# Attention scores on four 64x64 tiles of the TensorE array, with exchanged token quarters

## The reference, cut to what matters

```python
xn = _layernorm(x, axis=-1)
q = q * cos + _rotate_half(q) * sin          # positions 0..255 inside a batch
k = k * cos + _rotate_half(k) * sin
scores = jnp.einsum('bhsd,bhtd->bhst', q, k) / jnp.sqrt(jnp.float32(D))
causal = jnp.triu(jnp.full((S, S), -jnp.inf, dtype=jnp.float32), k=1)
probs = jax.nn.softmax(scores + causal[None, None], axis=-1)
out = jnp.einsum('bhst,bhtd->bhsd', probs, v)
...
g = _silu(_L0_ffn_ref(xn, ...))
x = x + s * g
```

## Time and profile before

| | |
|---|---|
| median of 3 runs | 303.01 us (302.92 to 303.16) |
| the profiled execution | 303.29 us, its span 301.5 us |
| TensorE matmul busy | 289.6 us, 96% of the span |
| ScalarE busy | 239.3 us, 79% |
| VectorE busy | 229.7 us, 76% |
| GpSimd busy | 213.5 us, 71% |
| granted TensorE clock | 1.00 of full speed |

### The profile page before, as it was taken

One profiled execution on the slowest core, in us unless ns is written; L12 is line 12 of the kernel. 1 busy time (PEld: TensorE's weight loads), 2 busy tenths in 40 slices (PEclk: granted clock), 3 DMA queues, 4 the chain that ended last, 5 costly groups with the idle time before them and its releaser, 6 DMA issues.

```text
span 301.5 us, 8603 instructions
## 1 busy us (share of the span) xinstructions
PE 289.6 (96%) x2362; PEld 235.0 (78%) x2362; DVE 229.7 (76%) x909; ACT 239.3 (79%) x863; POOL 213.5 (71%) x325
## 2 busy tenths in 40 slices
PE   8798999999999999999999989999999999999994
PEld 2576888888888888777776779999977778887663
DVE  4889998987777898988898723444377889898981
ACT  4278789898887889989998676677787898999971
POOL 2478878697778669999999982333226899998730
PEclk9999999999999999999999999999999999999999
DMA  6864685879333233444333382000234243543410
GB/s 192 249 133 115 114 276 148 205 194 300 87 75 68 60 75 83 107 101 102 90 97 90 112 245 55 2 0 2 66 93 108 64 113 99 121 106 109 113 37 17
DMA packets 39596, 33.35 MB, mean 111 GB/s; under 512 B 4801, under 2 KB 36674, under 8 KB 39554
## 3 DMA queue, kind: packets, MB, share of 16 engines
q1 hardware_dynamic: 38098, 30.51, 39.8%
q0 software_dynamic: 1024, 2.10, 2.4%
q10 hardware_dynamic: 432, 0.23, 0.3%
HBM read 11.07 MB, written 4.98 MB: 53 GB/s over the span
## 4 chain that ended last, share of the span: by engine, by line
PE 64%; POOL 14%; DVE 9%; issue 6%; DMA 3%; ACT 1%; POOLq 0%; SPq 0%; DVEq 0%; ACTq 0%
PE bank L1199 9%; PE bank L1187 9%; PE bank L1216 8%; PE bank L1450 7%; PE bank L1438 6%; PE bank L1233 6%; POOL probs L499 5%; POOL staged L488 5%; PE bank L1161 3%; DVE rot_out L617 3%; PE bank L1218 3%; PE bank L1189 3%; POOL xn L515 3%; DMA qk_sb<-staged 3%; DVE masked L633 2%
## 5 line engine op out<-in xcount | busy, mean ns | idle before, releaser
L975 ACT ACTIVATE pexp<-masked,negmax 128x128 f32<-128x128 f32 (+1 forms) x256 | 113.9, 452 | 2.2 <-DVE negmax L633 2.2
L499 POOL TENSOR_SCALAR probs<-pexp,rden 128x128 f32<-128x128 f32 (+1 forms) x195 | 84.3, 447 | 27.0 <-DVE rden L640 25.2
L633 DVE CUSTOM_DVE_ANT_0 masked<-bank,mask 128x128 f32<-128x128 f32 (+1 forms) x256 | 75.9, 352 | 21.4 <-PE bank L1189 20.5
L488 POOL TENSOR_TENSOR staged<-rot_out 128x512 f32<-128x512 f32 x56 | 71.4, 1278 | 16.2 <-DVE rot_out L617 15.6
L617 DVE TENSOR_TENSOR rot_out<-bank,rot 128x1024 f32<-128x1024 f32 x64 | 77.7, 1215 | 4.6 <-PE bank L1163 3.5
L997 ACT COPY probsT<-bank 128x384 f32<-128x384 f32 x126 | 54.0, 480 | 27.3 <-PE bank L1199 26.0
L1199 PE MATMUL bank<-ident,probs 128*128 128x128 f32 x384 | 54.0, 275 | 0.7 <-issue 0.5
L975 ACT ACTIVATION_READ_ACCUMULATOR pexp<-masked,negmax 128x1 f32 x256 | 50.0, 195 | 0.0
L1187 PE MATMUL bank<-qk_sb 64*128 64x256 f32 x256 | 47.0, 428 | 1.7 <-DMA qk_sb<-staged 1.3
L1199 PEld LDWEIGHTS bank<-ident,probs 128*128 128x128 f32 x384 | 43.0, 140 | 3.4 <-issue 1.2
L1233 PE MATMUL bank<-vo_sb,ctxT 128*128 128x128 f32 x256 | 37.8, 278 | 0.7 <-ACT ctxT L1004 0.7
(11 more groups left out here) (117 smaller groups left out, 483.6 us busy)
## 6 DMA issues: line engine op xcount, KB each, us to landing
qk_sb<-staged SPq DMA_DIRECT2D x128, 128.0 KB
w_sb<-in_w SPq DMA_DIRECT2D x2, 1024.0 KB, 5.8
w_sb<-in_w SPq DMA_DIRECT2D x4, 512.0 KB, 5.3
sorted_x<-z SPq DMA_DIRECT2D x1, 1408.0 KB, 8.0
sorted_g<-z SPq DMA_DIRECT2D x1, 1152.0 KB, 5.5
out<-res SPq DMA_DIRECT2D x8, 128.0 KB, 2.3
x_sb<-in_x SPq DMA_DIRECT2D x3, 256.0 KB, 3.8
rot<-in_c_rot SPq DMA_DIRECT2D x1, 512.0 KB, 5.7
```

The lines of the kernel that those rows point to most:

```text
L488: pool.tensor_tensor(staged[:, n % 2, :, m % 2, :], rot_out[:, m % 2, :, 0:S], rot_out[:, m % 2, :, S:2 * S], op=ALU.add).then_inc(staged_ ...
L499: pool.tensor_scalar(probs[:, g % 2, i, c], pexp[:, g % 2, i, c], rden[:, g % 2, i, k:k + 1], 1.0, ALU.mult, ALU.mult).then_inc(probs_read ...
L633: t = dve.tensor_tensor_reduce(masked[:, g % 2, i, c], s_bank[i][:, c], mask[:, c], -1.0, -NEG * 1e8, ALU.add, ALU.min, negmax[:, g % 2, i ...
L975: e = act.activation(pexp[:, g % 2, i, c], masked[:, g % 2, i, c], ACT.Exp, bias=negmax[:, g % 2, i, k:k + 1], scale=-1.0, accum_out=rowsu ...
```

## The change

The queries of each token tile are cut in quarters of 64 tokens, and the second tile's two quarters change places everywhere: `TOKEN_ORDER` says that positions 0 to 255 of a batch hold tokens of the quarters 0, 1, 3, 2. The rotary table and the mask follow that order, `x` is loaded and the result stored through it (`quarter_rows`), and softmax and sums over keys don't depend on it. `scores(g)` for g > 0 then issues five parts for each of the two heads in place of two, each on a 64x64 tile of the array: the row half is the head, the column half is the quarter's place in its tile. Column half 0 gets quarters 2 and 0 of the positions, with 256 and 64 keys; column half 1 gets quarters 3 and 1, with 128 + 64 and 128 keys (`SCORE_PARTS`). So each tile of the array streams 320 columns, where it was 384. What is left unwritten in PSUM is masked. Step 0 keeps the old form.

```diff
+Q = P // 2
+TOKEN_ORDER = (0, 1, 3, 2)
+SCORE_PARTS = ((2, slice(0, S)), (3, slice(0, P)), (1, slice(0, P)), (3, slice(P + Q, S)), (0, slice(0, Q)))
...
-    ang = np.arange(S, dtype=f)[None, :] * np.tile(inv, HPG)[:, None]
+    token = (np.array(TOKEN_ORDER)[:, None] * Q + np.arange(Q)).reshape(-1)
+    ang = token.astype(f)[None, :] * np.tile(inv, HPG)[:, None]
...
+        def quarter_rows(dram, part):
+            q = dram.rearrange("b (q p) c -> p b q c", p=Q)
+            return q[:, :, part::3 - 2 * part][:, :, 0:2]
...
                 def rows_in(u):
-                    n = slice(*TURNS[u])
-                    sp.dma_start(x_sb[:, n, :], xv[:, n, :]).then_inc(x_in[u], 16)
+                    for b in range(TURNS[u][0] // 2, TURNS[u][1] // 2):
+                        for part in range(2):
+                            sp.dma_start(x_sb[part * Q:part * Q + Q, 2 * b:2 * b + 2, :],
+                                         quarter_rows(x, part)[:, b]).then_inc(x_in[u], 16)
...
             def store(k):
...
-                sp.dma_start(out[b].rearrange("(n p) c -> p n c", p=P),
-                             res[:, k % 2].rearrange("p (n c) -> p n c", c=C)).then_inc(out_done[k % 2], 16)
+                for part in range(2):
+                    sp.dma_start(quarter_rows(out, part)[:, b],
+                                 res[part * Q:part * Q + Q, k % 2].rearrange("p (n c) -> p n c", c=C)
+                                 ).then_inc(out_done[k % 2], 16)
...
-                for i, r in enumerate(half_rows):
-                    wait(pe, masked_ready, 2 * g - 1 + i if g else 0)
-                    pe.matmul(s_bank[i][:, P:SW], qk_sb[r, 0, p, P:S], qk_sb[r, 1, p, :], start=True, stop=True)
-                for i, r in enumerate(half_rows):
-                    m = pe.matmul(s_bank[i][:, 0:P], qk_sb[r, 0, p, 0:P], qk_sb[r, 1, p, 0:P], start=True, stop=True)
+                for k, (q, keys) in enumerate(SCORE_PARTS):
+                    c = half_rows[q % 2]
+                    at = q // 2 * P
+                    for i, r in enumerate(half_rows):
+                        if k == 0:
+                            pe.wait_ge(masked_ready, 2 * g - 1 + i)
+                        m = pe.matmul(s_bank[i][c, at + keys.start:at + keys.stop], qk_sb[r, 0, p, q * Q:q * Q + Q],
+                                      qk_sb[r, 1, p, keys], start=True, stop=True)
                 m.then_inc(scores_done, 1)
```

More of the change, by code:

```diff
@@ L100, in host_constants @@
         "c_ident": np.eye(P, dtype=f),
-        "c_mask": np.where(k[None, :] > k[:, None], f(NEG), f(0.0)).astype(f),
+        "c_mask": np.stack([np.where(q[None, :] > q[:, None], f(NEG), f(0.0)) for q in (token[:P], token[P:])], 1).astype(f),
         "c_before": (k[:, None] < k[None, :]).astype(f),
@@ L391, in start @@
             def start():
-                xv = x.rearrange("b (n p) c -> p (b n) c", p=P)
                 def rows_in(u):
-                    n = slice(*TURNS[u])
-                    sp.dma_start(x_sb[:, n, :], xv[:, n, :]).then_inc(x_in[u], 16)
+                    for b in range(TURNS[u][0] // 2, TURNS[u][1] // 2):
+                        for part in range(2):
+                            sp.dma_start(x_sb[part * Q:part * Q + Q, 2 * b:2 * b + 2, :],
+                                         quarter_rows(x, part)[:, b]).then_inc(x_in[u], 16)
                 rows_in(0)
@@ L406, in start @@
                         sp.dma_start(rot[:], c_rot).then_inc(rot_in, 16)
-                sp.dma_start(mask[:, 0:P], c_mask).then_inc(m_in, 16)
-                sp.dma_start(mask[:, 2 * P:3 * P], c_mask).then_inc(m_in, 16)
+                sp.dma_start(mask[:, 0:P], c_mask[:, 0, :]).then_inc(m_in, 16)
+                sp.dma_start(mask[:, 2 * P:3 * P], c_mask[:, 1, :]).then_inc(m_in, 16)
                 sp.dma_start(wv_sb, w_vup).then_inc(w_in, 16)
@@ L477, in _ @@
             for i in range(2):
-                sp.wait_ge(out_done[i], 16 * B // 2)
+                sp.wait_ge(out_done[i], 32 * B // 2)
         @block.gpsimd
@@ L656, in stats @@
                 tiles = range(*TURNS[u])[first:last]
-                dve.wait_ge(x_in[u], 16)
+                dve.wait_ge(x_in[u], 16 * (TURNS[u][1] - TURNS[u][0]))
                 for n in tiles:
@@ L841, in add_rows @@
                 k = FINAL_ORDER.index(b)
-                wait(dve, out_done[k % 2], 16 * (k // 2))
+                wait(dve, out_done[k % 2], 32 * (k // 2))
                 dve.tensor_tensor(res[:, k % 2], gated[:], x_sb[:, 2 * b:2 * b + 2, :].rearrange("p n c -> p (n c)"),
@@ L1184, in scores @@
                 pe.wait_ge(qk_in[p], 32 * (g // NP) + 32)
-                for i, r in enumerate(half_rows):
-                    wait(pe, masked_ready, 2 * g - 1 + i if g else 0)
-                    pe.matmul(s_bank[i][:, P:SW], qk_sb[r, 0, p, P:S], qk_sb[r, 1, p, :], start=True, stop=True)
-                for i, r in enumerate(half_rows):
-                    m = pe.matmul(s_bank[i][:, 0:P], qk_sb[r, 0, p, 0:P], qk_sb[r, 1, p, 0:P], start=True, stop=True)
+                if g == 0:
+                    for i, r in enumerate(half_rows):
+                        pe.matmul(s_bank[i][:, P:SW], qk_sb[r, 0, p, P:S], qk_sb[r, 1, p, :], start=True, stop=True)
+                    for i, r in enumerate(half_rows):
+                        m = pe.matmul(s_bank[i][:, 0:P], qk_sb[r, 0, p, 0:P], qk_sb[r, 1, p, 0:P], start=True, stop=True)
+                    m.then_inc(scores_done, 1)
+                    return
+                for k, (q, keys) in enumerate(SCORE_PARTS):
+                    c = half_rows[q % 2]
+                    at = q // 2 * P
+                    for i, r in enumerate(half_rows):
+                        if k == 0:
+                            pe.wait_ge(masked_ready, 2 * g - 1 + i)
+                        m = pe.matmul(s_bank[i][c, at + keys.start:at + keys.stop], qk_sb[r, 0, p, q * Q:q * Q + Q],
+                                      qk_sb[r, 1, p, keys], start=True, stop=True)
                 m.then_inc(scores_done, 1)
```

## The result

| | before | after |
|---|---|---|
| median | 302.97 us (302.43 to 303.73, 6 runs) | 305.71 us (305.48 to 305.95, 6 runs) |
| profiled execution, span | 303.29, 301.5 | 305.83, 304.1 |

The change made the kernel slower: ratio 1.0091, 95% interval [1.0076, 1.0106]. The forecast was 300.1 us, its range 297.3 to 304.5.

What follows compares the result with a forecast made beforehand. TensorE was taken to lead the chain except where GpSimd holds it (113 to 165 us, gather stage). Terms -2.4 - 0.14 - 0.14 - 0.7 - 0.4 + 0.5 + 0.35 = -2.9 gave 300.1 us, range 297.3 to 304.5.

Steps and rivals of the forecast that it cites:

- The score group: TensorE's score matmuls of one step: 0.71 us in place of 0.85, 0.14 us less per step.
- rival 1: GpSimd's stretches: the gain goes on there; 295.1 us if all 63 groups count, 297.6 with half the held ones; a tenth.
- rival 3: Score groups: column halves with matmuls of unlike length don't run side by side; 0.92 us per group, 305.8 to 308.3; 0.15.
- rival 4: Score groups: TensorE's queue can't issue forty in 0.6 us; group of 1.1 to 1.2 us, over 315 us; 0.05.
- The sum of the score terms, -3.8: All score groups counted on the chain, without the transfers' fixed costs of 0.85 us: 3.8 us saved.
- forecast 2.4: Steps 5 to 22, 33 to 103 us: 18 groups at 0.14 are 2.52, less 0.1 lost to VectorE, so -2.4 us.
- rival 2: Early stretch: VectorE or transfers take up between half and all of the 2.4 us; 301.8 to 303.0 us; a tenth.
- forecast 0.7 and 0.14: Steps 42 to 46 save 5 x 0.14 = 0.7 us; of steps 40 and 41, before the experts, one group counts, 0.14.
- The gather stage to 280 us: 0: GpSimd's gathers, from 235.42 us to 280.57: GpSimd has no waits to give back, so nothing gained or lost.
- the start, +0.5: First loads of `x`, weights and rotary table: later by the halved transfers' extra issues, +0.5 us, bounds 0 and +1.0.
- The later loads of x ... 0: SyncE's queue: nine more issues, about 0.5 us each, on a queue that waits for GpSimd there; cost 0.
- the end, +0.35: Last store: the second half goes out one issue later with half the bytes; +0.35 us, bounds 0.2 and 0.5.

Runs made afterwards that it cites:

- experiment 15: Experiment 3's kernel unchanged (whole transfers, eight matmuls on 64x64 tiles, short part last), as control on another chip: 299.19 us, 0.9882 of the kernel before.
- experiment 10: Experiment 3's kernel once more (whole transfers, eight matmuls on 64x64 tiles in all steps), on another chip: 302.39 us, 0.9989 of the kernel before.
- experiment 4: The changed kernel with the old four score matmuls from step 42 on: 303.84 us, 1.0033 of the kernel before.
- experiment 12: Experiment 8's kernel once more (64x64 tiles, gathers replaced by additions, gates not brought back), on another chip: 300.40 us, 0.9917 of the kernel before.
- experiment 3: The kernel before with eight score matmuls per step on 64x64 tiles, query rows exchanged only in PSUM and put back by the transposes, whole transfers: 302.30 us, 0.9987.
- experiment 9: The changed kernel once more, on another chip: 305.42 us, 1.0095 of the kernel before.
- experiment 18: The changed kernel once more, on one more chip: 305.57 us, 1.0107 of the kernel before.
- experiment 1: The changed kernel with the four score matmuls of before, keeping the token order and halved loads and stores: 305.12 us, 1.007 of the kernel before.
- the mixed form: Experiment 3's kernel with the four matmuls of before in steps 46 to 61, the 64x64 form in all others: 300.18 and 299.95 us on two chips.
- experiment 2: The kernel before with only the ten score matmuls of the change, leaving out some scores; transfers and token order as before: 302.74 us, 0.9992.
- experiment 11: Experiment 5's kernel once more (form of before in steps 46 to 61), on another chip: 299.95 us, 0.991 of the kernel before.
- experiment 5: Experiment 3's kernel with the four matmuls of before in steps 46 to 61, the 64x64 form in all others: 300.18 us, 0.9908 of the kernel before.
- experiment 8: Experiment 3's kernel with each gather replaced by an addition on GpSimd, gates not brought back: 300.69 us, 0.9923 of the kernel before.
- experiment 13: Experiment 3's kernel with its four parts in the other order, so the 256-key matmul raises the semaphore: 299.53 us, 0.9876 of the kernel before.
- experiment 14: Experiment 3's kernel with one more matmul per step, on a 64x128 tile, that raises the semaphore: 314.61 us, 1.0381 of the kernel before.
- experiment 16: Experiment 13's kernel once more (256-key part last), on another chip: 299.33 us, 0.9888 of the kernel before.
- experiment 17: The changed kernel with its five parts in the other order, the 256-key part last: 304.45 us, 1.0057 of the kernel before.
- experiment 6: The kernel before with each long score matmul cut in two by its keys, on the old 64x128 tiles: 317.83 us, 1.0506.

## Why the prediction was wrong

**Right.** The score group: 0.71 us, -0.14, as worked out. GpSimd's rounds in the scatter stage stayed at 3.45 us (scatters start at 135.81, 139.26 and 142.72), so rival 1 was wrong. Rivals 3 and 4 were wrong: four tiles run side by side, also with matmuls of unlike length, and head 1's first record starts 0.007 us behind head 0's. The Trainium skill (TensorE: Matmul & The Clock Gate, Part 3, "What overlaps and what doesn't") has matmuls start and end strictly in program order; this trace does not agree, since by that rule, as rival 3 worked it out, the group would be 0.92. The sum of the score terms, -3.8, was right too where signals were not late: experiment 15 is 3.65 us faster than the kernel before. Its parts lay elsewhere. From the start of step 5 to that of step 23, 1.8 us came in there and in experiment 10 (forecast 2.4): twelve steps were shorter by 0.14 to 0.16, the other six by next to nothing, a weak form of rival 2. Steps 23 to 26 gave another 0.6, where the forecast had 0, and step 27 took 0.5 of it back. From step 1 to step 41 it came to 2.4 (forecast 2.5 to 2.7), and the stage behind step 48 gave 1.1 (forecast 0.4). That the sum agrees so well is in part luck, as its parts were off both ways. From step 41 to 48 the changed kernel gains 0.87 (forecast 0.7 and 0.14).

**Wrong: "The gather stage to 280 us: 0", and the gain behind it.** From step 48 to 63 the changed kernel goes from -0.76 to +2.01, where the forecast had -0.4. This 2.8 us is the larger part of the miss. I had argued that GpSimd holds that stage and so nothing changes; none of the rivals asked how soon VectorE hears of the scores. Shown are the place and the two conditions (experiments 4 and 12), that the signals come behind the end of the `DMA_INDIRECT`, and that it differs from one chip to another (3 and 10 against 15). Not shown is the mechanism, nor whether the shape of the tiles or the number of small records is what counts.

**Wrong: the start, +0.5.** It was +1.30, outside the bounds. The second half of `x` came 1.30 late. I had reckoned with one issue more, 0.49, and with a shorter way for half the bytes; the issue was 0.81 and the way 0.49 longer. The rotary table, from which the upper bound came, did not matter.

**Wrong: "The later loads of x ... 0".** The queue got 2.57 us behind at 35.12, and two waits of TensorE took 1.2 us of its lead. The size is not steady. In experiments 9 and 18, the same kernel, step 16 slipped by 0.52 and 0.47 us, step 8 by 0.26 and not at all; in experiment 4 only step 8 did. Step 8 goes in part with the issue of 1.55 us: experiment 4 has one of 1.67 and slips by 0.66; experiments 1 and 18 have none, their queue is free at 34.48 and 34.29, and step 8 does not slip. With the old form step 16 does not slip either (experiment 1 stays at +1.50), as TensorE comes later to it.

**Undersized: the end, +0.35.** The span says +0.57, experiment 1 +0.63, above the bound of 0.5.

Put together, in the changed kernel's trace: start 1.30, steps 2 to 27 -1.27 (the forecast's -2.5 less the two waits of 1.2), to step 41 +0.08, to 48 -0.87, to 63 +2.77, end +0.57. The sum is 2.58, and 303.29 + 2.58 = 305.87, the execution's 305.83.

## What to carry to other kernels

A shorter group of instructions on the busiest engine is worth what the next engine hears of it: check in the trace how long its signal takes in every stage, beside every kind of work of the other engines, before counting the gain. To exchange rows for a better layout on the array, do it where a matmul already passes over them (here the transposes, at no cost that the runs show) and not in the transfers, where it cost 2.3 us. And time such a change on more than one chip: the best kernel here, with the 64x64 form in all steps, gained 3.6 us on one and nothing that could be measured on two others; the mixed form gained 2.6 and 2.7 us, on one chip of each kind.

## What the runs showed of the hardware that was not expected

- With the 64x64 form, signals that TensorE raises while GpSimd runs an indirect DMA reached VectorE 0.1 to 1.1 us late on the chips of the changed kernel's three traces and of experiments 2 to 4 and 10 to 12; on those of experiments 5, 8 and 13 to 17 at most 0.2 us late, and nearly always not at all. In the nine traces that show it VectorE started 0.2 to 0.7 us after the indirect DMA's record on GpSimd had ended, whether the signal was raised 0.15 or 1.0 us into it. With the 128-column form a few were up to 0.2 us late, the others on time.
- The issue of a half transfer of `x` took 0.60 to 0.75 us on SyncE's queue (the last of the 16 took 1.55, 1.67 and 1.53 in the first trace of the changed kernel and in experiments 4 and 17), that of a half store 0.60 to 0.63. In the kernel before, with all 128 partitions, the loads of one batch took 0.44 and 0.43, the later ones of two batches 0.60 to 0.66, the first five stores 0.59 to 0.63 and the last three 0.37 to 0.38.
- Float32 records on one 64x128 tile started 0.11 us apart with 64 streamed columns as with 128 (experiment 6). Groups on 64x64 tiles keep ten matmuls of two heads in 0.71 us, but a single matmul on a 64x128 tile behind them added 0.37 (experiment 14).
- The five parts took 0.77 us in the order from short to long (experiment 17), and 0.71 from long to short; the four parts took 0.70 in both orders (experiments 15 and 16).
